# A graph layer's edge tiles cut to 127 edges, 837 row gathers in place of 830

## The reference, cut to what matters

```python
ea = edge_attr @ W_edge.T + b_edge
msg = jax.nn.relu(x[src] + ea)
aggr = jax.ops.segment_sum(msg, dst, num_segments=N_NODES)
h = (1.0 + eps) * x + aggr
h = jax.nn.relu(h @ W1.T + b1)
return h @ W2.T + b2
...
h = jnp.maximum(_layernorm(x, axis=-1), 0.0)
x = x + _L0_gnn_ref(h, edge_index, edge_attr_96, ...)
```

## Time and profile before

| | us |
|---|---|
| median of 3 runs | 1237.12 |
| lowest, highest | 1236.62, 1238.39 |
| the profiled execution: its span, first to last instruction | 1239.1 |

### The profile page before, as it was taken

The page is one execution under the profiler, slowest core; times in us unless marked ns, Lnnn a source line. Parts: engine busy times, 40 slices in busy tenths (PEclk is TensorE's granted clock), DMA queues, the critical chain, the costliest instruction groups (busy, mean ns, idle before and its releaser), DMA issues.

```text
span 1239.1 us, 9124 instructions
## 1 busy us (share of the span) xinstructions
PE 628.9 (51%) x2786; PEld 515.6 (42%) x2786; DVE 518.5 (42%) x658; ACT 193.0 (16%) x233; POOL 785.9 (63%) x838
## 2 busy tenths in 40 slices
PE   2226544455554454555554555444555545554568
PEld 2215434344433334444444444343444434443456
DVE  6645344444433333354344333333343444333373
ACT  5102111111111111111111111111111111111114
POOL 6756666666666666666666666666666666666540
PEclk9999666665656665565665656655556565565668
DMA  8513222333222223333333332222222333232212
GB/s 217 145 33 94 66 64 67 74 85 74 67 67 67 68 67 75 72 73 75 74 93 95 76 74 66 67 67 67 64 66 68 74 88 72 68 67 61 49 29 78
DMA packets 51183, 93.30 MB, mean 75 GB/s; under 512 B 17722, under 2 KB 20443, under 8 KB 51136
## 3 DMA queue, kind: packets, MB, share of 16 engines
q0 software_dynamic: 26592, 40.85, 16.3%
q1 hardware_dynamic: 24390, 51.63, 15.2%
q10 hardware_dynamic: 154, 0.24, 0.1%
HBM read 87.85 MB, written 4.80 MB: 75 GB/s over the span
## 4 chain that ended last, share of the span: by engine, by line
another core or an unknown queue 56%; DVE 23%; issue 8%; DVEq 8%; PE 3%; DMA 1%; ACT 0%; SPq 0%; ACTq 0%
DVE edge_ps L854 7%; DVE edge_ps L865 5%; DVE msg_parts L879 4%; DVEq L768 3%; DVE acc L759 2%; DVEq L770 2%; DVE acc L849 1%; PE edge_ps L601 1%; DVEq L762 1%; DVE stats L639 1%; PE edge_ps L462 1%; DVEq L795 1%; DVE select L705 1%; DVEq L783 1%
## 5 line engine op out<-in xcount | busy, mean ns | idle before, releaser
L352 POOL DMA_INDIRECT gathered<-h_table,src_all x810 | 764.5, 944 | 396.4 <-issue 234.7
L462 PE MATMUL edge_ps<-w_edge,edge_in 97*128 97x96 f32 x1660 | 403.6, 392 | 521.4 <-issue 517.1
L462 PEld LDWEIGHTS edge_ps<-w_edge,edge_in 97*128 97x128 f32 x1660 | 361.8, 302 | 565.0 <-issue 564.1
L787 DVE TENSOR_REDUCE sums<-agg_ps 128x192 f32<-128x576 f32 x41 | 31.0, 757 | 590.4 <-remote 590.4
L424 ACT ACTIVATE msg_parts<-edge_ps 128x960 bf16<-128x960 f32 (+1 forms) x83 | 79.2, 957 | 970.1 <-DVE edge_ps L865 704.4
L543 PE MATMUL agg_ps<-msg_parts,select 128*128 128x288 bf16 x816 | 167.9, 386 | 6.4 <-issue 6.4
L705 DVE TENSOR_TENSOR select<-const_ps,dst_rel 128x2560 bf16<-128x2560 f32 (+1 forms) x43 | 120.8, 2812 | 34.8 <-issue 28.5
L543 PEld LDWEIGHTS agg_ps<-msg_parts,select 128*128 128x128 bf16 x816 | 109.4, 134 | 60.9 <-issue 8.1
L865 DVE TENSOR_TENSOR edge_ps<-edge_ps,gathered 128x960 f32<-128x960 f32 (+1 forms) x83 | 90.9, 1141 | 47.9 <-remote 42.8
L854 DVE SCALAR_TENSOR_TENSOR edge_ps<-edge_ps,msg_parts 128x960 f32<-128x960 f32 (+1 forms) x83 | 91.1, 1144 | 0.3 <-issue 0.3
L879 DVE TENSOR_TENSOR msg_parts<-edge_ps,msg_parts 128x960 bf16<-128x960 f32 (+1 forms) x83 | 90.8, 1136 | 0.3 <-issue 0.3
(11 more groups left out here) (73 smaller groups left out, 143.1 us busy)
## 6 DMA issues: line engine op xcount, KB each, us to landing
edge_in<-edge_t_dram SPq DMA_DIRECT2D x165, 240.0 KB
gathered<-h_table,src_all POOLq DMA_INDIRECT x810
x_all<-x_dram SPq DMA_DIRECT2D x5, 420.0 KB
h_all<-x_dram SPq DMA_DIRECT2D x10, 210.0 KB
out_dram<-h_all SPq DMA_DIRECT2D x10, 210.0 KB
h_table<-h_all SPq DMA_DIRECT2D x3, 420.0 KB
h_table<-h_all SPq DMA_DIRECT2D x1, 630.0 KB
dst_by_row<-dst_rows_dram SPq DMA_DIRECT2D x1, 480.0 KB, 4.2
```

Of the source, the lines that this page charges most:

```text
L352: nc.gpsimd.indirect_dma_start(out=gathered[c % SLOTS][:, at:at + D], out_offset=None, in_=table, in_offset=bass.IndirectOffsetOnAxis(ap=s ...
L462: mm = pe.matmul(edge_bank(c, g)[:, (k - k0) * D:(k - k0 + 1) * D], edge_in[c % SLOTS][:, k * EDGE_TILE:(k + 1) * EDGE_TILE], w_edge[:], s ...
```

## The change

EDGE_TILE goes from 128 to 127. There are then 836 tiles and a tail of 78 edges. Every tensor with an edge on each partition has 127 partitions (`src_all`, `dst_all`, `dst_rel`, `gathered`, `msg_parts`, `select`, `edge_ps` and others), and so every DMA, gather and instruction on them. A group of 5 tiles loads 635 columns of edge features in place of 640. LAST_SIDES goes from (8, 5, 2) to (10, 5, 3), so that there are 41 batches of 20 tiles, one of 10 and one of 6. The number of batches and the order of the work stay.

```diff
-EDGE_TILE = 128
+EDGE_TILE = 127
...
-LAST_SIDES = (8, 5, 2)
+LAST_SIDES = (10, 5, 3)
...
-        src_all = sb("src_all", [128, TILES + 1], I32)
-        dst_all = sb("dst_all", [128, TILES + 1], I32)
-        dst_rel = sb("dst_rel", [128, TILES + 1 + MOST])
+        src_all = sb("src_all", [EDGE_TILE, TILES + 1], I32)
+        dst_all = sb("dst_all", [EDGE_TILE, TILES + 1], I32)
+        dst_rel = sb("dst_rel", [EDGE_TILE, TILES + 1 + MOST])
         edge_in = [sb(f"edge_in{b}", [D + 1, MOST * EDGE_TILE]) for b in range(SLOTS)]
-        gathered = [sb(f"gathered{b}", [128, MOST * D]) for b in range(SLOTS)]
-        msg_parts = [sb(f"msg_parts{b}", [128, MOST, SPLIT, D], BF16) for b in range(2)]
-        select = [sb(f"select{b}", [128, MOST, WINDOW], BF16) for b in range(2)]
+        gathered = [sb(f"gathered{b}", [EDGE_TILE, MOST * D]) for b in range(SLOTS)]
+        msg_parts = [sb(f"msg_parts{b}", [EDGE_TILE, MOST, SPLIT, D], BF16) for b in range(2)]
+        select = [sb(f"select{b}", [EDGE_TILE, MOST, WINDOW], BF16) for b in range(2)]
...
-        edge_ps = [psum(f"edge_ps{p}", [128, 2 * BANK]) for p in range(PAIRS)]
+        edge_ps = [psum(f"edge_ps{p}", [EDGE_TILE, 2 * BANK]) for p in range(PAIRS)]
...
+        edge_iota = const_ps[0:EDGE_TILE, 0:WINDOW]
...
-                    iota_ps.unsqueeze(1).broadcast_to((128, tiles, WINDOW)),
-                    dst_rel[:, bass.ds(at, tiles)].unsqueeze(2).broadcast_to((128, tiles, WINDOW)),
+                    edge_iota.unsqueeze(1).broadcast_to((EDGE_TILE, tiles, WINDOW)),
+                    dst_rel[:, bass.ds(at, tiles)].unsqueeze(2).broadcast_to((EDGE_TILE, tiles, WINDOW)),
```

More of the change, by code:

```diff
@@ L119, in gnn_layer @@
         stats = sb("stats", [NP, COLS, 6])
-        raw_stats = sb("raw_stats", [128, SIDES * SIDE_TILES, 6])
+        raw_stats = sb("raw_stats", [EDGE_TILE, SIDES * SIDE_TILES, 6])
         LN_ALL = COLS + SIDES * SIDE_TILES
@@ L141, in gnn_layer @@
         bounds_i = sb("bounds_i", [1, 5 * BOUND_ROWS // 2], I32)
-        src_all = sb("src_all", [128, TILES + 1], I32)
-        dst_all = sb("dst_all", [128, TILES + 1], I32)
-        dst_rel = sb("dst_rel", [128, TILES + 1 + MOST])
+        src_all = sb("src_all", [EDGE_TILE, TILES + 1], I32)
+        dst_all = sb("dst_all", [EDGE_TILE, TILES + 1], I32)
+        dst_rel = sb("dst_rel", [EDGE_TILE, TILES + 1 + MOST])
         edge_in = [sb(f"edge_in{b}", [D + 1, MOST * EDGE_TILE]) for b in range(SLOTS)]
-        gathered = [sb(f"gathered{b}", [128, MOST * D]) for b in range(SLOTS)]
-        msg_parts = [sb(f"msg_parts{b}", [128, MOST, SPLIT, D], BF16) for b in range(2)]
-        select = [sb(f"select{b}", [128, MOST, WINDOW], BF16) for b in range(2)]
-        late_select = {c: sb(f"late_select{c}", [128, tiles_of[c] + (c == LAST), WINDOW]) for c in (LATE, LAST)}
+        gathered = [sb(f"gathered{b}", [EDGE_TILE, MOST * D]) for b in range(SLOTS)]
+        msg_parts = [sb(f"msg_parts{b}", [EDGE_TILE, MOST, SPLIT, D], BF16) for b in range(2)]
+        select = [sb(f"select{b}", [EDGE_TILE, MOST, WINDOW], BF16) for b in range(2)]
+        late_select = {c: sb(f"late_select{c}", [EDGE_TILE, tiles_of[c] + (c == LAST), WINDOW]) for c in (LATE, LAST)}
         sums = sb("sums", [WINDOW, SIDES, D])
@@ L416, in _ @@
                 act.wait_ge(raw_var_ready, k + 1)
-                nc.scalar.activation(std[:, cols], spread2[:, cols], ACT.Sqrt,
-                                     bias=eps_col[:], scale=1.0 / D).then_inc(raw_std_done, 1)
+                nc.scalar.activation(std[0:EDGE_TILE, cols], spread2[0:EDGE_TILE, cols], ACT.Sqrt,
+                                     bias=eps_col[0:EDGE_TILE, :], scale=1.0 / D).then_inc(raw_std_done, 1)
             for c in range(LATE):
@@ L680, in raw_var @@
                 ordered(last)
-                combine(raw_stats[:, k0:k1, :], COLS + k0, k1 - k0, 128).then_inc(raw_var_ready, 1)
+                combine(raw_stats[:, k0:k1, :], COLS + k0, k1 - k0, EDGE_TILE).then_inc(raw_var_ready, 1)
             def raw_normalise(k):
@@ L685, in raw_normalise @@
                 dve.wait_ge(raw_std_done, k + 1)
-                ordered(scale_and_shift(COLS + k0, k1 - k0, 128))
+                ordered(scale_and_shift(COLS + k0, k1 - k0, EDGE_TILE))
                 for n in range(k0, k1):
@@ L689, in raw_normalise @@
                     col = COLS + n
-                    last = nc.vector.tensor_scalar(tile, tile, rstd[:, col:col + 1], shift[:, col:col + 1],
+                    last = nc.vector.tensor_scalar(tile, tile, rstd[0:EDGE_TILE, col:col + 1], shift[0:EDGE_TILE, col:col + 1],
                                                    ALU.mult, ALU.add)
@@ L806, in make_late_select @@
                 nc.vector.tensor_tensor(
-                    late_select[c][:], iota_ps.unsqueeze(1).broadcast_to((128, tiles, WINDOW)),
-                    dst_rel[:, first_tile[c]:first_tile[c] + tiles].unsqueeze(2).broadcast_to((128, tiles, WINDOW)),
+                    late_select[c][:], edge_iota.unsqueeze(1).broadcast_to((EDGE_TILE, tiles, WINDOW)),
+                    dst_rel[:, first_tile[c]:first_tile[c] + tiles].unsqueeze(2).broadcast_to((EDGE_TILE, tiles, WINDOW)),
                     ALU.is_equal).then_inc(late_selected[c], 1)
```

4 lines of the change are left out of this document (2 added, 2 removed).

## The result

| | before | after |
|---|---|---|
| median, us | 1237.76 | 2435.96 |
| lowest to highest, us | 1236.62 to 1238.65 | 2435.59 to 2440.15 |
| span of the profiled execution, us | 1239.1 | 2438.1 |

The changed kernel takes 1.968 times as long (95% interval 1.965 to 1.971). The forecast was 1255 us and its range ended at 1300 us: it was wrong. What came is the kind of thing that the rival left out of the range describes, "a gather gets much dearer on POOL", though that was priced at 1980 us.

The account below looks back on a forecast made before the run. The prediction took the number of gathers times their price as the bound. 1239.1 + 8.4 (six gathers) + 9 (index loads) + 0.6 (last batch) = 1257, less 2 us from span to median: 1255 us, range 1095 to 1300.

Parts of the forecast that it names:

- What bounds the kernel now: Whole kernel: bound by the number of gathers times their price, 1.40 us each, not by any engine's busy time.
- PE's hold: PE's queue at each batch's end: PE goes on only after 1.394 us for each gather issued; POOL and DVE wait.
- the price of a gather of 127 rows: Each tile gather: price taken as fixed, 0 us change, with -9 us kept in case it goes by rows.
- Rival (2): POOL's gathers: 127 rows on one engine are 126 steps of 9 ns, 2.02 us each, 1980 us; chance 0.15.
- POOL works along a list, one long list is no dearer: POOL's gathers: argument against the much dearer gather, that one long list costs no more than 16 short ones.
- Six more gathers, +8.4: Last batches, 16 to 20 and 4 to 6 gathers: six more at 1.40 us, all on the path, +8.4 us.
- +0.6 for the last batch: Last batch: two more fp32 tiles and a few more columns on DVE and ACT, +0.6 us.
- The index loads, +9: Source index loads at the start: 127 partitions may use one DMA engine, delaying POOL; +9 us, bounds 0 and 16.
- (1): PE's hold goes away or shrinks, POOL's 1.25 us a gather becomes the bound: 1104 us; chance 0.25.
- (3): Gathers on one DMA engine land later and skew the queues: +29 us, 1284 us; chance 0.10.
- (4): Only the count changes, with the gather price by rows: 1246 us with the loads' delay, 1237 without; chance 0.12.
- What would show it: List of trace signs: batch distance, POOL's mean gather (944 or 2,000 ns), POOL's restart, packets per gather, PE queue's pace.

Follow-up runs that it names:

- e7: Kernel of before, unchanged, run once more with its own trace: 1244.31 us.
- e12: Kernel of before, with batches 3 to 38 issuing only their first 20 down to 1 gathers, four batches per count: 831.40 us beside 1079.32.
- e9: The whole change with tiles of 117 edges in place of 127: 1443.46 us where the kernel of before takes 1245.
- e3: Kernel of before, but gathers after batch 1 take 127 rows, 128 partitions everywhere else: 2345.05 us, ratio 2.174 to before.
- e5: Changed kernel with tiles of 127 edges, but gathers padded to 128 rows, the last unused: 1087.94 us, ratio 1.0080 to before.
- e2: Kernel of before, gathering only 128, 112, 64, 16, 126, 120, 125, 96 or 110 rows per tile, four batches each: 1094.53 us.
- e11: Kernel of before, gathering only 128, 117, 120, 104, 110, 96, 78, 119 or 48 rows per tile, four batches each: 1092.56 us.
- e4: Kernel of before, with the three index loads each cut into 127 partitions and 1: 1091.53 us, ratio 1.0114 to before.
- e6: Changed kernel, with each gather cut in two, of 112 and 15 rows, and source loads cut alike: 2085.36 us, ratio 1.9326 to before.
- e1: Kernel of before, with the 20 gathers of each of batches 3 to 40 taking 20 different row counts, 128 to 16: 1253.28 us.

## Why the prediction was wrong

**What bounds the kernel now.** "The number of gathers times their price" was right in form. The price of 1.39 us was that of PE's hold, which is there in some sets of runs and not in others: a batch takes 1.43 us a gather in e7, 1.25 in e12. The prediction took it for a trait of the kernel. That it is issued gathers that hold PE rests on the readings of the earlier trace rows and two of e9, of 40 and 14 gathers; in all of them tiles, loads and matmuls grow with the gathers, and the runs that would part them met no hold. So it is argued and not shown, and what the hold is stays open. For the changed kernel it doesn't matter.

**The step that failed: the price of a gather of 127 rows.** It was taken as unchanged, with bounds of -9 and 0 us; "Both ends suppose that 127 rows are spread and described as 128 are". POOL's time went from 944 to 2553 ns. e3 puts this one step at 1266 us for 790 gathers, and e5, which takes it back for all, at 1348, all of the loss but 8 us. The neighbour row (128 rows, 944 ns) was near in number and far in kind. The bounds were drawn from rows per gather, while the price goes by rows per engine, 8 and 127.

**The rule that bore on it.** The Trainium skill ("DMA: Bandwidth & Descriptors", section "Why a DMA increments its semaphore by 16 and not by 1") was cited for the loads and said to hold for GpSimd's DMAs too, and then no term was moved by it for the gathers. The traces agree with its largest divisor up to 16 for both: the packets of gathers of 16 to 128 rows in e2 and e11, and the load of 127 rows that takes 18.8 us in e4. The exception that the section makes for some direct copies did not apply to these indirect ones: 127 rows left as one list.

**Rival (2), much dearer on POOL.** The mechanism was right: steps of one row on one engine, 126 more. It gave 2.02 us and 1980 in all; measured were 2.55 us and 2436. The step was mis-sized at 9 ns, from 944 - 881 over 7. The runs show (2553 - 944) / 119 = 13.5 ns on one engine and 15 ns on 16. The 881 ns of the tail's 10 rows are 42 ns above the 839 of 16 rows in e2, one row per engine in both, and 42 ns over seven steps are the 6 ns that were missing. Ten rows cost more than sixteen as do the other sizes on fewer than 16 engines in e2, e11 and e6 (15 rows, 877 ns); the reason for that is open. The error is that of a slope drawn between two near points, one of which was of another kind, and carried 18 times as far.

**Its chance.** 0.15, and the range, 1095 to 1300 us, was drawn without it. Of the two cases against which it was weighed, "POOL works along a list, one long list is no dearer" had no row at all behind it. The range was narrowed to the part of the outcomes that has a fine price, and left out the one with a coarse one.

**Six more gathers, +8.4, and +0.6 for the last batch.** e5: +8.2 us, 7.5 for six gathers at 1.25 each and 0.7 for the rest. The count and the rest were right; that the first term is so near is in part luck, since its 1.40 us was the hold's price and e5 had none. In the changed kernel the six cost 17.

**The index loads, +9.** e4: +12.8 us alone, within the 11 to 16 of the one-engine case. (The stores behind the load in SP's queue are 1.68 MB; the 1.9 MB of the prediction count ACT's in, which changes its bound by under 1 us.) In the changed kernel nothing, since POOL reaches the wait 32 us later than in the earlier trace rows.

**Rivals (1), (3), (4).** (1), one list per gather leaves little to hold PE: no hold shows in the changed kernel, but POOL had become slower than it would be, so whether it shrank can't be told, and nothing was gained. (3), landings skewed by one engine: a gather lands 6.8 us after its issue, where 2.5 is the median in e5; since POOL sets the pace, that can lengthen only the end of the kernel. (4) supposed the price by the total of rows. For POOL's own time e1 and e2 exclude it; for the hold it was not tested, and e9's 1.41 us at 117 rows speaks against it (by rows 1.27).

**What would show it.** The prediction's own list named it: POOL's mean per gather, 944 ns or 2,000 under (2), and the packets per gather. Both were the first lines to read.

No version of these beats the kernel of before: 128 rows have the lowest price per row of all sizes in the sweeps, and every other size needs more gathers.

## What to carry to other kernels

Before the partition count of a DMA is changed, take its largest divisor up to 16 and divide by it: what counted for GpSimd's indirect gathers here (rows of 384 B) is the number of rows in the longest list, at about 14 ns each over 0.83 us, and a prime count like 127 or 113 puts all in one list. If a tile must have an awkward number of rows, pad the DMA to the next good one and ignore the rest (e5: 1088 us, where e3's gathers of 127 rows take 2345 with nothing else changed, and the changed kernel 2436). When a change moves an operation to a form that the trace doesn't hold, the nearest number is no neighbour if the form decides; keep the unpriced case inside the range.
